# Three tiles of the first expert laid into the last three attention rounds, and the second expert's weights loaded in twelve pieces

## The reference

```python
def _layernorm(x, axis=-1, eps=1e-05):
    m = jnp.mean(x, axis=axis, keepdims=True)
    v = jnp.var(x, axis=axis, keepdims=True)
    return (x - m) / jnp.sqrt(v + eps)

# attention, H = 16 heads, D_K = 16
qh = proj(q, w_q, b_q); kh = proj(k, w_k, b_k); vh = proj(v, w_v, b_v)
scores = jnp.einsum('bhqd,bhkd->bhqk', qh, kh) / jnp.sqrt(jnp.float32(D_K))
attn = jax.nn.softmax(scores, axis=-1)
ctx = jnp.einsum('bhqk,bhkd->bhqd', attn, vh)
return jnp.einsum('bsd,ed->bse', ctx, w_o) + b_o      # ctx with its heads put side by side again

# experts, NUM_EXPERTS = 8, TOP_K = 2, D = 256, F = 1024
probs = jax.nn.softmax((x @ router_w).astype(jnp.float32), axis=-1)
top_w, top_i = jax.lax.top_k(probs, TOP_K)
cw = jnp.zeros((T, NUM_EXPERTS)).at[jnp.arange(T)[:, None], top_i].set(top_w)
for e in range(NUM_EXPERTS):
    h = jax.nn.silu(x @ gate_w[e]) * (x @ up_w[e])
    out = out + cw[:, e:e + 1] * (h @ down_w[e])

# the whole
x = x + attention(_layernorm(x), ctx_1024, ctx_1024, ...)
x = x + experts(_layernorm(x), ...)
```

## Time and profile before

| | us |
|---|---|
| median of 3 runs | 978.39 (977.79 to 980.58) |
| profiled execution | 976.2 |
| its span, first to last instruction | 974.4 |
| PE busy | 875.0 (90%) |
| DVE busy | 621.6 (64%) |
| ACT busy | 468.9 (48%) |
| POOL busy | 290.0 (30%) |

### The profile page before, as it was taken

One profiled execution on the slowest core, in us unless ns is written; L12 is line 12 of the kernel. 1 busy time (PEld: TensorE's weight loads), 2 busy tenths in 40 slices (PEclk: granted clock), 3 DMA queues, 4 the chain that ended last, 5 costly groups with the idle time before them and its releaser, 6 DMA issues.

```text
span 974.4 us, 32193 instructions
## 1 busy us (share of the span) xinstructions
PE 875.0 (90%) x12208; PEld 781.1 (80%) x12208; DVE 621.6 (64%) x1930; ACT 468.9 (48%) x891; POOL 290.0 (30%) x337
## 2 busy tenths in 40 slices
PE   2899789999999761799999999999999999999995
PEld 1667667777777541789999999999999999999995
DVE  7788858888988544457547447545745746544443
ACT  3677757788878551335335334333523534323321
POOL 5556643344343325012112112212211112211111
PEclk9998979999999775899999999999999999999999
DMA  4321123222224312152522522522332352222221
GB/s 136 112 57 42 60 66 90 67 85 65 89 67 147 104 45 95 51 180 35 162 56 44 152 53 37 160 33 52 103 88 56 66 152 35 33 33 34 33 33 17
DMA packets 69073, 73.57 MB, mean 75 GB/s; under 512 B 19725, under 2 KB 62811, under 8 KB 69019
## 3 DMA queue, kind: packets, MB, share of 16 engines
q1 hardware_dynamic: 44666, 32.94, 11.7%
q0 software_dynamic: 12944, 17.87, 10.7%
q10 hardware_dynamic: 11408, 22.06, 6.4%
HBM read 45.18 MB, written 26.39 MB: 73 GB/s over the span
## 4 chain that ended last, share of the span: by engine, by line
PE 50%; issue 6%; DMA 6%; DVE 3%; ACT 3%; POOL 1%; SPq 0%; POOLq 0%; another core or an unknown queue 0%; ACTq 0%; DVEq 0%
PE bank L483 11%; PE bank L485 11%; PE bank L484 11%; PE bank L681 5%; PE bank L683 5%; PE bank L682 5%; DMA raw<-expert_rows 4%; DMA expert_rows<-rows,slot_u 2%; PE bank L656 1%; POOL expert_rows L1388 1%; PE bank L544 1%; DVE h_full L1252 1%; ACT h_hi L830 1%; DVE h_lo L1258 1%; ACT pt_hi L758 1%
## 5 line engine op out<-in xcount | busy, mean ns | idle before, releaser
L483 PE MATMUL bank<-xg,e_hi 128*128 128x128 f16 x2176 | 372.7, 219 | 0.7 <-DVE xg L1229 0.6
L484 PE MATMUL bank<-xg,e_hi 128*128 128x128 f16 x2176 | 372.7, 219 | 0.0
L485 PE MATMUL bank<-xg,e_lo 128*128 128x128 f16 x2176 | 372.7, 219 | 0.0
L1419 POOL DMA_INDIRECT out<-y_sb,tok_row x68 | 113.4, 1668 | 466.0 <-DVE y_sb L1247 442.5
L483 PEld LDWEIGHTS bank<-xg,e_hi 128*128 128x128 f16 x2176 | 213.4, 98 | 2.0 <-issue 0.8
L484 PEld LDWEIGHTS bank<-xg,e_hi 128*128 128x128 f16 x2176 | 213.4, 98 | 0.8
L485 PEld LDWEIGHTS bank<-xg,e_lo 128*128 128x128 f16 x2176 | 213.4, 98 | 0.0
L828 ACT ACTIVATE g_act<-bank 128x512 f32<-128x512 f32 x136 | 81.3, 598 | 249.1 <-PE bank L485 230.2
L1252 DVE SCALAR_TENSOR_TENSOR h_full<-bank,g_act 128x512 f32<-128x512 f32 x136 | 94.0, 691 | 129.3 <-ACT g_act L828 121.6
L681 PE MATMUL bank<-e_hi,h_hi 128*128 128x256 f16 x544 | 148.4, 273 | 3.8 <-DVE h_lo L1258 3.8
L682 PE MATMUL bank<-e_lo,h_hi 128*128 128x256 f16 x544 | 148.3, 273 | 0.0
(11 more groups left out here) (175 smaller groups left out, 1766.2 us busy)
## 6 DMA issues: line engine op xcount, KB each, us to landing
raw<-expert_rows SPq DMA_DIRECT2D x68, 132.5 KB, 2.6
e_stage<-in_gate_w ACTq DMA_DIRECT2D x7, 1024.0 KB
e_stage<-in_up_w ACTq DMA_DIRECT2D x7, 1024.0 KB
e_stage<-in_down_w ACTq DMA_DIRECT2D x7, 1024.0 KB
expert_rows<-pads SPq DMA_DIRECT2D x8, 530.0 KB
xin<-in_x SPq DMA_DIRECT2D x16, 256.0 KB, 2.8
xres<-in_x SPq DMA_DIRECT2D x16, 256.0 KB
out<-x SPq DMA_DIRECT2D x16, 256.0 KB
```

The source lines that it names most:

```text
L483: pe.matmul(dst, a_hi(c), b_hi(c), start=c == 0, stop=False)
L484: pe.matmul(dst, a_hi(c), b_lo(c), start=False, stop=False)
L485: mm = pe.matmul(dst, a_lo(c), b_hi(c), start=False, stop=ends and c == chunks - 1)
L1419: pool.indirect_dma_start(out, bass.IndirectOffsetOnAxis(tok_row[:], 0), y_sb[:], None, compute_op=ALU.add).then_inc(added, 16)
```

## The change

Rounds 18 to 20 are no longer made by `batches` with the common body: each engine has a function `last_rounds(c, r, z)` with c = 15, r = 14, z = 13, in which the rest of attention and tiles 0, 1 and 2 of expert 0 stand in one order written by hand. The expert phase starts with tile 3.

- The first 384 rows of expert 0's region are filled with padding early, and from batch 11 on `next_row` of expert 0 is at least 384, so later rows fall behind these three tiles. With the inputs here this moves nothing, since 402 rows are there by then.
- The weights of expert 1 are loaded by SP in twelve DMAs of 256 KB, each issued when the one before has landed, with the loads of `raw` and the stores of x2 between them. `load_next` on ACT goes.
- Weights of expert e+1 are split in tiles 2 and 3 of expert e, three pieces a step, instead of in tiles 0 to 2 with two. The load of expert e+2 follows after tile 3, and ACT waits for it ahead of tile 2 of the next expert instead of ahead of tile 0.
- `rows` gets a third buffer, for batch 15. The scatters count on two semaphores; in the draining rounds each now waits for the one two before it, where before the four of a batch went out together.
- ACT fetches its tables of Silu and Exp by a dummy activation (`fetch`) ahead of use.

```diff
-PIECES_AT = (0, 2, 4, 6, 8, 10, 12)
-PREPARING = 3
+PIECES_AT = (0, 3, 6, 9, 12)
+PREPARING = 2
+LOADING = 2
+AHEAD = 3
+HELD_FROM = 11
...
-        def batches(eng, body, in_between=None):
+        def batches(eng, body, last_rounds):
...
-            if in_between:
-                in_between()
-            for first in range(B, B + STAGES - 1):
+            for first in range(B, B + 2):
                 body(*[At(first - stage) if first - stage < B else None for stage in range(STAGES)])
+            last_rounds(At(B - 1), At(B - 2), At(B - 3))
...
         @block.sync
             spread_keys(At(B - 1))
+            sp.wait_ge(e_lo_ready, PIECES)
+            load_second(range(0, 3))
+            landed(sp, At(HELD_FROM))
+            load_rows(0)
+            store_c(At(B - 3))
+            load_c(At(B - 2))
+            load_second(range(3, 7))
+            store_c(At(B - 2))
+            load_c(At(B - 1))
+            load_second(range(7, 9))
+            load_rows(1)
+            load_second(range(9, CHUNKS))
+            store_c(At(B - 1))
+            load_rows(2)
...
         @block.tensor
+            def last_rounds(c, r, z):
+                front, back = range(FS // 2), range(FS // 2, FS)
+                pe.wait_ge(q_lo_ready, KC * B)
+                turn_rows(0)
+                weigh_values(c, c.plus % 2, UNITS - 2)
+                ranks(z)
+                gate_up(0, 0, 0, front)
+                weigh_values(c, c.plus % 2, UNITS - 1)
+                gate_up(0, 0, 0, back)
+                turn_att(c)
+                turn_x2(r, r.plus % 2)
+                gate_up(0, 0, 1, front)
+                project_o(c)
+                router(r)
+                turn_rows(1)
+                gate_up(0, 0, 1, back)
+                down(0, 0, 0, 0, front)
+                ranks(r)
+                down(0, 0, 0, 0, back)
+                gate_up(1, 0, 0)
+                pe.wait_ge(h_ready, STEPS)
+                gate_up(1, 0, 1, front)
+                turn_x2(c, rows_at(c))
+                down(1, 0, 1, 1)
+                router(c)
+                turn_rows(2)
+                gate_up(1, 0, 1, back)
+                ranks(c)
+                down(1, 0, 0, 0)
+                gate_up(2, 0, 0)
+                down(2, 0, 1, 1)
+                gate_up(2, 0, 1)
+                down(2, 0, 0)
+                pe.wait_ge(tables_ready, 3)
+                down(3, 0, 1, 1)
...
         @block.scalar
-                prepare = PREPARING if e + 1 < E else 0
-                if prepare:
-                    act.wait_ge(e_in, 48 * (e + 2))
+                prepare = LOADING + PREPARING if e + 1 < E else 0
...
         @block.gpsimd
+            def last_rounds(c, r, z):
+                make_rows(r, rows_at(r))
+                scatter(z, rows_at(z), 2)
+                scatter(r, rows_at(r), 2, range(0, 1))
+                make_rows(c, rows_at(c))
+                scatter(r, rows_at(r), 2, range(1, 4))
+                pool.wait_ge(x2_out, 16 * B)
+                add(0)
+                scatter(c, rows_at(c), 0)
```

More of the change, by code:

```diff
@@ L282, in build @@
         row_ready = sem("row_ready")
-        scattered = sem("scattered")
+        scattered = [sem(f"scattered{n}") for n in range(2)]
         x2_out = sem("x2_out")
@@ L455, in _ @@
                     pad_expert(e + 1)
-                with sp.Fori(1, n) as j:
+                with sp.Fori(1 if e else AHEAD + 1, n) as j:
                     at = sp.snap(e * REGION + j * TILE)
@@ L657, in turn_rows, with gate_up @@
                 mm.then_inc(xg_turned, 1)
-            def gate_up(g, parity, s):
-                if s == 0:
+            def gate_up(g, parity, s, part=range(FS)):
+                if s == 0 and part[0] == 0:
                     pe.wait_ge(xg_ready, g + 1)
-                for k in range(FS):
+                for k in part:
                     f = s * FS + k
@@ L670, in gate_up, with down @@
                                    lambda c: xg[:, c, 0, :], lambda c: xg[:, c, 1, :], KC)
-                mm.then_inc(gu_made, 1)
-            def down(g, parity, s, back=0):
+                if part[-1] == FS - 1:
+                    mm.then_inc(gu_made, 1)
+            def down(g, parity, s, back=0, part=range(FS)):
                 pe.wait_ge(h_lo_ready, g * STEPS + (s + 1 - back * STEPS))
-                if s == 0:
+                if s == 0 and part[0] == 0:
                     after(pe, y_ready, g)
-                for k in range(FS):
+                for k in part:
                     f = s * FS + k
@@ L704, in _ @@
                 pe.wait_ge(e_lo_ready, (e + 1) * PIECES)
-                tile(first, parity, 1 - parity, e > 0, True)
-                with pe.Fori(1, rest if last else counts[e]) as j:
+                tile(first if e else AHEAD, parity, 1 - parity, e > 0, True)
+                with pe.Fori(1 if e else AHEAD + 1, rest if last else counts[e]) as j:
                     tile(pe.snap(first + j), parity, parity, True, True)
@@ L1375, in make_rows, with scatter @@
                 after(pool, token_ready, j.value(1, 1))
-            def scatter(r, par, n):
+            def scatter(r, par, apart_by, part=range(2 * NT)):
+                if r.reg is None and r.plus == 0:
+                    pool.wait_ge(pad_ahead, 16)
                 after(pool, row_ready, r.value(2, 2))
@@ L1401, in body, with add @@
                 if z:
-                    scatter(z, z.plus % 2, n)
+                    scatter(z, z.plus % 2, 1 if n else 2)
                 if pieces := early_pieces(n):
                     split_expert(pieces)
-            batches(pool, body)
-            pool.wait_ge(x2_out, 16 * B)
-            pool.wait_ge(tables_ready, 3)
-            total = 0
-            for e in range(E):
-                total = pool.snap(total + tile_count(pool, e))
-            with pool.Fori(0, total) as g:
+            def add(g):
                 pool.wait_ge(added, g * 16 + 16)
@@ L1420, in _, with last_rounds @@
                                         y_sb[:], None, compute_op=ALU.add).then_inc(added, 16)
+            def last_rounds(c, r, z):
+                make_rows(r, rows_at(r))
[6 more added lines that the diff above has]
+                scatter(c, rows_at(c), 0)
+            batches(pool, body, last_rounds)
+            pool.wait_ge(tables_ready, 3)
+            total = 0
+            for e in range(E):
+                total = pool.snap(total + tile_count(pool, e))
+            with pool.Fori(1, total) as g:
+                add(g)
 def kernel(**inputs):
```

228 lines of the change are left out of this document (173 added, 55 removed).

## The result

| | before | changed |
|---|---|---|
| median, same chip, us | 978.09 (977.69 to 980.58) | 955.69 (954.68 to 958.58) |
| profiled execution | 976.2 | 956.3 |
| its span | 974.4 | 954.5 |

A forecast was written before the change was run, and what follows sets the result against it. Expert phase bound by PE's unbroken matmuls, with idle PE ahead of it. Terms -26.6 + 1.0 - 0.5 = -26.1 take 976.2 to 950.1; the median lies 2.2 above, hence 952. Forecast 947 to 957 (chance 0.55), range 943 to 965.

The forecast's parts named there:

- three tiles in PE's 28.8 idle us: Last rounds, 353 to 395 us: three tiles of 24.6 us fit into PE's idle time there.
- The start moves from 357.2 to 352.2: Start of last rounds, ranks(13): without the large load's delay to a scatter, 5 us gained, bounds 0 and 8.
- The laid-in work makes the chain 4 us longer: Ranks(13) to ranks(15): 29 us instead of 25.3, because tile work is inserted between attention's steps.
- the three steps: Ranks(13) to residual(15) 11.5 us, on to high_rows(15) 9.5, on to ranks(15) 8.0; before 8.6, 9.4 and 7.2.
- in come: Residual(15) to high_rows(15), on DVE: added copy to xg 0.6 us, weights and slots 2.0, one combine 0.7.
- In all 14.7 us: Ranks(15) to tile 3's gate_up: DVE's work, PE's steps and weight pieces sum to 14.7 us, bounds 13 and 19.
- I take 0.15 us for each of seven experts: Expert phase, tiles 2 and 3: a third weight piece per step on DVE costs 1.0 us in all, bounds 0 to 6.
- The other loads move one tile later and meet the same kind of raw loads: 0: Expert phase: moving the other expert weight loads one tile later was said to cost nothing.
- the 0.5 us forecast as gained on raw: Second expert, 427 to 443 us: ACT no longer waits for the load, raw is less delayed; 0.5 us gained.
- Rival D: Expert phase: preparing in two tiles makes DVE or ACT the bound, 18 us lost, 969 us in all; chance 0.06.
- C: Last three rounds: PE stays at half clock, so the kernel takes 981.6 us, slower than before; chance 0.03.
- Table loads at 0: ACT, ahead of the last router exponentials: table load is hidden and costs 0, or 1.3 us if uncovered.

The follow-up runs named there:

- pieces_only: Kernel before, with only expert 1's load changed to twelve 256 KB transfers issued by SP; 966.34 us against 970.04, ratio 0.9957.
- warm_before: Kernel before, with unread matmuls filling PE's waits in the last three rounds to hold its clock up; 969.14 us against 970.04, ratio 0.9993.
- free_first: Changed kernel, but before the last rounds the first of the scatters set apart goes without its wait; 956.87 us, ratio 0.9783 to before.
- y_later: Changed kernel, with POOL's add of tile 0's output moved behind the last batch's four scatters; 952.22 us, ratio 0.9815 to before.
- late_y: Changed kernel, tile 0's add behind the last scatters, load behind tile 4's first Silu step in experts 1 to 5; 949.28 us, ratio 0.9781 to before.

## Why the prediction was right, and where its steps were not

- The mechanism, three tiles in PE's 28.8 idle us: right; tile 3 started at 396.4 for 395.9, not behind the DMA of raw, as forecast. It stood behind DVE's copy, also as forecast, but the copy itself had waited 2.31 us for PE.
- "The start moves from 357.2 to 352.2": the term was right (4.65 us by the copies, 3.7 to 4.2 by pieces_only). The 3 us missing lay ahead of it, in executions that differ by more than that before 190 us. Nothing behind the pieces was late: residual(14) waits 0.84 us for PE in both kernels, not for xres.
- "The laid-in work makes the chain 4 us longer": wrong, it was 3.7 shorter. The mis-sized terms are the three steps: 11.5 was 8.9, 9.5 was 6.3 and 8.0 was 6.4. In the middle step the two waits that go were sized right (forecast 2.1 and 1.1, measured 2.1 and 1.0); the term that failed is "in come" 3.3 us of copy, weights, slots and combine, which cost nothing. In the first step 4.0 us of gate_up were added in full, though PE had been idle 3.9 of the 12 us there and took some of it in. In the last, the scatter's 1.0 us is there (POOL begins the rows of batch 15 0.9 us behind the start of high_rows, 0.1 before), and the step is shorter all the same; full clock gives 0.4 of it (6.8 in warm_before, 7.2 in pieces_only), and no run shows the rest.
- "In all 14.7 us" to tile 3: it was 19.4, out of its bounds (13 to 19). On the chip without the standstill it was 16.7 to 17.3, so that accounts for about 2 of the 4.7. For the rest the sum had DVE as the late one, and at the end it is PE, which reads the last five tile counts ahead of the turn: 2.3 us by DVE's wait. Before, these readings hid in a wait of 10.95 us. The sum had no term for them; no run moved them.
- "I take 0.15 us for each of seven experts" for the third piece, and "The other loads move one tile later and meet the same kind of raw loads: 0": the second is the step that failed. The sum did not ask what stands behind the three DMA issues on ACT and their wait for DVE's third low part. It is Silu, then DVE's h_lo, then PE: about 3 to 4 us in all. The third piece alone, in expert 6, costs nothing that shows. The bounds of the first term, 0 to 6, would have held it. Nor did the 0.5 us forecast as gained on raw come: its waits stayed the same.
- Rival D was not the bound: of the preparing tiles only tile 3 delays PE, by 0.73 us at the next gate_up. C didn't come: from 358 to 390 the clock is 1.00.
- Table loads at 0: right. In the changed kernel ACT ends the x2t copy, loads a table and goes on at once:

```profile
373.84 1.02 ACT L860 ACTIVATE x2t<-bank 128x1024 f16<-128x1024 f16 x1 [0.77 <-PE bank L651]
374.88 1.28 ACT L928 ACT_TABLE_LOAD   x1
376.17 0.20 ACT L928 ACTIVATE seed<-ident 1x1 f32<-1x1 f32 x1
```

ACT was busy until the load and again 0.01 us behind it: 1.30 us for the change. The Trainium skill, "ScalarE: Activation LUTs", What ACT_TABLE_LOAD costs, counts 1.38 us more for a drain; this trace has no room for it.

The median came out 3.7 us above 952: +3.2 for the start, -2.7 for chain and tail together and +5.7 for the expert phase are 6.2 for the profiled execution; from that go 2.5, since this execution lay 0.6 us above its median and the forecast was put 1.9 above its own sum. An error of -7.4 us in the chain cancelled most of those of +3.2 and +4.7 beside it, so the closeness of the number is in part luck.

## What to carry to other kernels

Fill an engine's idle stretch with work of the next phase when both run in order on separate chains; short laid-in instructions can cost nothing where they fall into gaps of the old order, and the chain itself can get shorter if a new order and a third buffer take waits out of it and the filler brings the clock back. When a step is moved, list each DMA issue that goes with it and the first compute instruction behind it on that engine: here three pieces and three issues ahead of a Silu ate 3 to 4 us of 26, and one compute step between wins them back. Look also for readings of registers in an engine's queue that a long wait used to hide. Before reordering around a single buffer (y_sb), ask who waits for its release.

## What was not expected of the hardware

- ACT and DVE stood still together for over 4 us at 381 to 386, PE partly, with no releaser in the trace. The changed kernel on both chips where before took some 978 us and free_first there have it on ACT (4.78, 4.84, 4.83); none of the four kernels on the chip with 970.5 has, nor have y_later and late_y on the one with 970.0. Its cause is open.
- The kernel before took 978.1, 970.5, 978.6 and 970.0 us on four chips, up to 0.9% apart, while its runs on one chip spread by 0.3 to 0.6%. Times from different chips can't be compared where 0.5% matters.
